# A graph transformer layer on one core: query exponentials straight from PSUM, count windows regrouped, second-layer weights rounded in pieces

## The chip, the cores and the metric

The kernel runs on one core of one Trainium2 chip. The metric is the time of one execution on the device in microseconds (us), lower is better.

## The reference

x is 1250 nodes of 768 features; 40000 edges with a source, a destination and one of three relations. All is float32. Cut to what matters:

```
xn = layernorm(x)
# relational graph attention, twice; layer 1 has 4 heads of 192, layer 2 has 1 of 768
xr = einsum('nd,rdf->rnf', x, W);  qi = xr[etype, dst] @ q;  kj = xr[etype, src] @ k
alpha = leaky_relu(qi + kj, 0.2)
e = exp(alpha - segment_max(alpha, dst)[dst]);  a = e / (segment_sum(e, dst)[dst] + 1e-16)
out = segment_sum(a * xr[etype, src], dst) + b
gnn = layer2(elu(layer1(xn)))
# linear attention of 12 heads of 64
q, k, v = xn @ W_qkv + b_qkv;  phi(x) = where(x > 0, x + 1, exp(x))
kv = sum_n phi(k) v^T;  y = phi(q) kv / max(phi(q) . sum_n phi(k), 1e-6)
mix = y @ W_out + b_out
x = x + gnn + mix
# int8 feed-forward
x = x + (clip(round(layernorm(x) / 0.02), -128, 127) @ weight_t) * 0.0002 + bias
```

## The kernel before

The nodes are ten blocks of 128 rows, the last one short; the features are six slices of 128 (`K6`). A float32 product is made of three float16 ones: each operand is split in a high part, made on ACT, and a low part, made on DVE, and a product of one block with 384 columns (`CW`) is 6 slices x 3 = 18 matmuls. The graph is turned into counts: for each relation, source and destination the number of edges, kept as 60 **count windows** of 21 destinations. A window is a chain of 14 matmuls of one-hot matrices (`count_window`, L1824), whose one-hots DVE builds in pairs (`one_hots`, L1345 and L1346, seven pairs a window); ACT copies the counts out of PSUM (`window_out`, L956) and SP stores them. First tile and count of a window are registers that PE and DVE each load from a table in memory (`window`, L446 to L452). The windows are spread over the stages as filling work; with the windows, `wq_tile` (L1885, 12 small matmuls) makes products of the graph weights with the attention vectors.

The stages in order: layernorm and transposes; K, then V (`W_K`, `W_V`; one window behind each product, L1824); K^T V (L1867); the **query stage**; a transition; the **y stage**; 20 **O products** (y @ W_out) followed by layer 1's products (both L1995), with masks and maxima beside them; layer 1's aggregation (L2044); **layer 2**'s 60 products in six chunks m = 0 to 5 (L1811 to L1813); its aggregation (L2101, L2102); the feed-forward.

The order within a stage is written out by hand for each engine; semaphores tie the engines together.

Query stage: six groups, each of 128 query features of all nodes in four row groups of 320 (`NRG`, `RG`), one PSUM bank each. A group runs over six k; a k step is 12 matmuls of 320 columns (L1911). Windows stand ahead of k = 2, of k = 4 and behind the group; a tile ahead of some k. PE loads the registers of the group's three windows at its start. When a bank is full (`q_done`), DVE adds the bias into `q_t` (L1451) and frees the bank (`q_free`), ACT makes exp(min(q, 0)) by Relu and Exp (L994, L996), and DVE combines both into `QF` (L1456). In the second half of the stage DVE also adds `bsum` = bo + b2 to the rows of X (L1461, L1462), and SP stores these to `acc_d` in the y stage (L642), from where they are loaded as the addend of the O products (`load_o`, L510; added at L1508).

After the last group PE does that group's third window and one more, then the y stage: per block `weighted` (12 matmuls of phi(q) with kv, L1925), DVE's division (`normalised`, L1468, L1472, L1477), PE's transposes of the result (L1936) and the two float16 parts (ACT, and DVE at L1490). Blocks 0 to 7 have a window, each block a tile.

Layer 2: per product ACT writes the high part of the result (L1168), DVE the low part (L1668, which frees the bank); in m = 1 to 3 DVE also makes two maxima per pair of blocks (L1676, L1679). Weights are double buffered: `w_hi_part` (L937, ACT) at the end of chunk m rounds the weights of chunk m + 2 in one piece, having waited for their load (`w_in`), and `w_lo_part` (L1371, DVE) makes the low part of chunk m + 1 behind the first pair of m. The aggregation's weights (`exponentials2`, `weights_part`, POOL's `pl` at L921) begin after the last product.

## Time and profile before

| | us |
|---|---|
| median of 3 runs | 1757.9 (1757.42, 1757.9, 1764.39) |
| profiled execution, device time | 1760.24 |
| its span in the trace | 1758.5 |
| busy: PE | 1621.5 (92% of the span) |
| busy: DVE | 1308.4 (74%) |
| busy: ACT | 774.4 (44%) |
| busy: POOL | 138.1 (8%) |

The mean granted clock of TensorE is 0.966 of full speed, and 183.30 MB pass through the DMA queues. In the rows below a line of a timeline or of the chain begins with the start and the length in us; "[3.03 <-PE ps L1911]" means that the engine had been idle for 3.03 us and what ended that; in a list of waits the numbers are the total in us, how often, and the longest. Matmuls overlap in the pipeline, so the length of one is more than its share of PE; the distance of two starts is the time that the work between them took. "x14" joins fourteen instructions in one row.

### The profile page before, as it was taken

How to read it: one execution, taken by the hardware profiler on the slowest of the kernel's cores; microseconds unless marked ns; L12 is line 12 of the kernel's file. 1: busy time of each engine (PE TensorE's matmuls, PEld its weight loads, DVE VectorE, ACT ScalarE, POOL GpSimd, SP SyncE). 2: the span in 40 equal slices, each digit the busy share in tenths (PEclk: the TensorE clock that was granted, in tenths of full speed). 3: DMA queues.
4: the chain of work that ended last, by engine and by line, in shares of the span. 5: the costliest groups of instructions: out<-in, count | busy, mean ns of one | idle time of the engine just before them, and what ended most of it. 6: DMA issues, size and time to landing. Idle time of an engine off the chain costs nothing.

```text
span 1758.5 us, 34402 instructions
## 1 busy us (share of the span) xinstructions
PE 1621.5 (92%) x10547; PEld 1179.7 (67%) x10548; DVE 1308.4 (74%) x2631; ACT 774.4 (44%) x1021; POOL 138.1 (8%) x245
## 2 busy tenths in 40 slices
PE   4999999987999999889999999989889799999987
PEld 3566667766755666469999999986555455555544
DVE  8698875578749999248899898973664377777785
ACT  4331112222234555168888898863211133333342
POOL 2000000000000000000000000000000033333340
PEclk8999999999899999989999999989999999999999
DMA  5111133323557664541003132132654541011212
GB/s 197 32 58 59 61 73 117 102 79 98 163 157 236 195 194 150 154 128 59 30 30 116 61 110 61 51 98 79 196 171 150 182 154 53 1 53 53 65 55 88
DMA packets 130308, 183.30 MB, mean 104 GB/s; under 512 B 14934, under 2 KB 100088, under 8 KB 130220
## 3 DMA queue, kind: packets, MB, share of 16 engines
q1 hardware_dynamic: 130220, 182.17, 33.4%
q8 instruction: 49, 0.80, 0.2%
q14 instruction: 39, 0.32, 0.1%
HBM read 121.33 MB, written 60.81 MB: 104 GB/s over the span
## 4 chain that ended last, share of the span: by engine, by line
PE 75%; DVE 10%; issue 5%; DMA 3%; ACT 3%; DVEq 2%; POOL 1%; SPq 1%; ACTq 0%; POOLq 0%
PE ps L2044 22%; PE ps L1995 12%; PE ps L2102 7%; PE ps L2101 7%; PE ps L1811 5%; PE ps L1813 4%; PE ps L1812 4%; PE ps L1824 4%; PE ps L1911 2%; PE ps L1885 2%; DVE oh_q L1345 2%; DVE oh_p L1346 1%; PE ps L2113 1%; PE ps L1980 1%; DMA xr_d<-ev 1%
## 5 line engine op out<-in xcount | busy, mean ns | idle before, releaser
L2044 PE MATMUL ps<-xrh,pf 128*128 (+1 forms) x2400 | 399.9, 329 | 11.3 <-DVE pf L1622 11.3
L2044 PEld LDWEIGHTS ps<-xrh,pf 128*128 128x128 f32 x2400 | 393.5, 191 | 17.8 <-issue 15.4
L1811 PE MATMUL ps<-w_hi,xt_hi 128*128 128x384 f16 x600 | 199.6, 333 | 23.9 <-DVE ev L1668 15.4
L1345 DVE TENSOR_SCALAR oh_q<-pat,codeT,neg_w 125x630 f16<-125x630 uint16 x420 | 185.8, 442 | 41.3 <-PE ps L1824 29.7
L1618 DVE SCALAR_TENSOR_TENSOR vb<-vb,tb 128x1260 f32<-128x1260 f32 x120 | 172.9, 1467 | 54.7 <-ACT vb L1119 53.8
L2101 PE MATMUL ps<-x,ph 128*128 (+1 forms) x600 | 196.5, 327 | 16.8 <-POOL pl L921 10.8
L1622 DVE SCALAR_TENSOR_TENSOR pf<-vb,CT 128x1260 f32<-128x1260 f32 x120 | 175.8, 1468 | 35.3 <-PE ps L2044 35.3
L1812 PE MATMUL ps<-w_lo,xt_hi 128*128 128x384 f16 x600 | 199.2, 332 | 0.0
L1813 PE MATMUL ps<-w_hi,xt_lo 128*128 128x384 f16 x600 | 199.1, 332 | 0.0
L2102 PE MATMUL ps<-x,ph 128*128 (+1 forms) x600 | 197.9, 330 | 0.0
L1119 ACT ACTIVATE vb<-qbc,kcol 128x1260 f32<-128x1260 f32 x120 | 161.0, 1345 | 39.5 <-DVE pf L1622 38.1
L1529 DVE CUSTOM_DVE_ANT_0 tt_junk<-kbc,mb 126x1260 bf16<-126x1260 f32 x120 | 169.1, 1466 | 10.0 <-issue 10.0
L1114 ACT ACTIVATE tb<-qbc,kcol_leak 128x1260 f32<-128x1260 f32 x120 | 159.6, 1343 | 20.2 <-DVE vb L1618 18.9
L1824 PE MATMUL ps<-oh_q,oh_p 125*128 125x315 f16 x840 | 132.1, 304 | 23.7 <-DVE oh_p L1346 23.1
L1181 ACT ACTIVATE ph<-p 128x252 f16<-128x252 f32 x150 | 61.9, 413 | 161.5 <-PE ps L2102 158.5
L921 POOL TENSOR_TENSOR pl<-p,ph 128x252 f16<-128x252 f32 x150 | 111.1, 742 | 197.4 <-ACT ph L1181 186.0
L1995 PE MATMUL ps<-w_hi,xt_hi 128*128 128x384 f16 x360 | 118.9, 330 | 7.4 <-ACT ev L1043 7.4
L1824 PEld LDWEIGHTS ps<-oh_q,oh_p 125*128 125x128 f16 x840 | 80.9, 99 | 66.3 <-DVE oh_p L1346 20.1
L1995 PE MATMUL ps<-w_lo,xt_hi 128*128 128x384 f16 x360 | 118.7, 330 | 0.0
L1995 PE MATMUL ps<-w_hi,xt_lo 128*128 128x384 f16 x360 | 118.5, 329 | 0.0
L1668 DVE TENSOR_TENSOR ev<-ps,ev 128x384 f16<-128x384 f32 x60 | 32.8, 556 | 101.1 <-ACT ev L1168 97.9
L1811 PEld LDWEIGHTS ps<-w_hi,xt_hi 128*128 (+1 forms) x600 | 59.7, 99 | 68.7 <-issue 32.4
(235 smaller groups left out, 2451.1 us busy)
## 6 DMA issues: line engine op xcount, KB each, us to landing
qbc<-tq_d SPq DMA_DIRECT2D x12, 1260.0 KB, 6.6
wst<-in_L_gnn_W SPq DMA_DIRECT2D x60, 192.0 KB, 3.2
xr_d<-ev SPq DMA_DIRECT2D x60, 192.0 KB, 2.0
xrh<-xr_d SPq DMA_DIRECT2D x4, 2880.0 KB, 14.8
x_d<-ev SPq DMA_DIRECT2D x60, 192.0 KB, 2.3
mb_d<-mb SPq DMA_DIRECT2D x30, 310.1 KB
mb<-mb_d SPq DMA_DIRECT2D x30, 310.1 KB
x<-x_d SPq DMA_DIRECT2D x2, 3840.0 KB, 18.9
```

The costliest lines, as they stand in the source:

```text
L1345: dve.tensor_scalar(oh_q[0:ET, u, :], pat[0:ET, :], codes[:, k:k + 1], neg_w[0:ET, ds(w, 1)], ALU.subtract, ALU.is_equal)
L1529: dve.tensor_tensor_reduce(out=tt_junk[k][0:WK, :], in0=kbc[0:WK, h, :], in1=mb[w % 2][0:WK, :], scale=1.0, scalar=2 * BIG, op0=ALU.subtra ...
L1618: dve.scalar_tensor_tensor(vb[j][:, :], vb[j][:, :], 2.0, tb[j][:, :], ALU.min, ALU.max).then_inc(v_step, 1)
L1622: dve.scalar_tensor_tensor(pf[j][:, 0:ND].rearrange("p (w d) -> p w d", d=WN), vb[j][:, :].rearrange("p (w d) -> p w d", d=WN), 2.0, CT[:, ...
L1811: pe.matmul(ps[:, bank, 0:CW], a_hi, hi[:, k, :], start=(k == 0), stop=False)
L1812: pe.matmul(ps[:, bank, 0:CW], a_hi, lo[:, k, :], start=False, stop=False)
L1813: last = pe.matmul(ps[:, bank, 0:CW], a_lo, hi[:, k, :], start=False, stop=(k == K6 - 1))
L1824: last = pe.matmul(ps[:, bank + q, 0:QH], oh_p[0:ET, u, :], oh_q[0:ET, u, q * QH:(q + 1) * QH], start=start, stop=False, skip_group_check= ...
L1995: mm = pe.matmul(ps[:, 6 + n % 2, 0:CW], a[:, k, i * P:(i + 1) * P], w[:, k, :], start=(q % PM == 0), stop=(q % PM == PM - 1))
L2044: mm = pe.matmul(out[b], pf[j][:, b * DB:b * DB + P], x, start=(first and b % 2 == 0), stop=False, skip_group_check=True)
L2101: pe.matmul(ps[:, bank, 0:CW], p, cols(off, off + CW), start=start, stop=False, skip_group_check=True)
L2102: mm = pe.matmul(ps[:, bank + 1, 0:CW + n1], p, cols(off + CW, off + D + n1), start=start, stop=False, skip_group_check=True)
```

## The change

1. **Query exponentials.** ACT reads the PSUM bank itself: Relu(-q - bq), then Exp; DVE makes `QF` in one operation, max(q + (bq + 1), exp), and only this frees the bank (`q_out` in place of `q_free`). `q_m` has four buffers, `q_t` is gone. The identity used: phi(q) = max(q + 1, exp(min(q, 0))).
2. **Biases.** `bsum` and its additions to X are gone, and so are the ten stores of X and the waits for them. POOL splits bo + b2 in three bfloat16 rows, which go through memory (`ob_d`) to `orow`; a matmul of ones with these three rows stands ahead of each O product. `load_o` reads x.
3. **Windows and tiles.** A query group has four windows, ahead of k = 2, 4 and 5 and behind the group (24 in place of 19 before the y stage); three blocks of the y stage have one, eight before. At a k the tile now stands ahead of the window, and groups 1 to 5 begin with one.
4. **K and V.** DVE loads a window's registers ahead of the wait for the product.
5. **Layer 2's weights.** In m = 1 to 4, ACT rounds those of chunk m + 1 in three pieces of two slices, behind its pairs 0, 1 and 2; DVE makes the low pieces behind its pairs 1, 2 and 3. Nothing is rounded at a chunk's end.
6. **Last aggregation.** Its first weights are made by DVE, ACT and POOL in and right after the last pair of m = 5.

The diff, cut to its core:

```diff
-W_A = W_Q + 3 * K6 + 1
-
-Q_TILES = (0, 3, 8, 13, 18, 22, 26)
+W_A = W_Q + 4 * K6
+
+Q_TILES = (0, 2, 7, 12, 17, 22, 27)
...
 def block_tiles(i):
...
-    return range(Q_TILES[-1] + i, Q_TILES[-1] + i + 1)
+    return range(Q_TILES[-1] + i, min(Q_TILES[-1] + i + 1, WT_TILES))
...
 def step_tile(q, k):
...
-    t = Q_TILES[q + 1] - K6 + k
-    return range(t, t + 1) if t >= Q_TILES[q] else range(0)
-
-assert W_A + NB >= NWN and block_tiles(NB - 1)[-1] == WT_TILES - 1
+    t = Q_TILES[q] + (k - 3 if q == 0 else k)
+    return range(t, t + 1) if Q_TILES[q] <= t < Q_TILES[q + 1] else range(0)
...
-    sp.dma_start(oa[n % 4][:, :], acc_d[i * P:(i + 1) * P, c * CW:(c + 1) * CW]).then_inc(oa_in[n % 4], 16)
+    rows = P if i < NB - 1 else TAIL
+    sp.dma_start(oa[n % 4][0:rows, :], x[i * P:i * P + rows, c * CW:(c + 1) * CW]).then_inc(oa_in[n % 4], 16)
...
     chunk_load(7)
+    sp.wait_ge(ob_step, 6)
+    sp.dma_start(ob_d.rearrange("j (p c) -> p j c", c=K6), osplit[:, :, :]).then_inc(ob_st, 16)
     for q in range(K6):
-        for k in range(1, K6):
+        for k in range(K6):
             if k in (3, 5):
...
+                store_window(sp, W_Q + 4 * q + k // 2 - 1, cc_, (4 * q + k // 2 - 1) % 2)
             for t in step_tile(q, k):
                 wq_load(t + 3)
-        store_window(sp, W_Q + 3 * q + 2, cc_, (3 * q + 2) % 2)
-    store_window(sp, W_A - 1, cc_, (W_A - 1 - W_Q) % 2)
+        for u in (2, 3):
+            store_window(sp, W_Q + 4 * q + u, cc_, (4 * q + u) % 2)
+        if q == 0:
+            sp.wait_ge(ob_st, 16)
+            sp.dma_start(orow[:, :], ob_d[:, :]).then_inc(or_in, 16)
     for i in range(NB):
-        sp.wait_ge(xb_done, i + 2)
...
     pool.wait_ge(bias_in, 80)
-    pool.tensor_tensor(bsum[:, :], bsum[:, :], b2_bc0[:, :], ALU.add).then_inc(xb_done, 1)
+    pool.tensor_tensor(ocol[:, :], ocol[:, :], o2col[:, :], ALU.add).then_inc(ob_step, 1)
...
         k = w - W_Q
         window_out(w, 6, cc_, k % 2, k // 2 + 3 * NB // 2 + (1 if k % 2 else 2))

+    act.wait_ge(bq_done, 1)
     for c in range(2):
         for fb in range(3):
-            wa = W_Q + 3 * (3 * c + fb)
-            late_out(wa)
-            late_out(wa + 1)
+            wa = W_Q + 4 * (3 * c + fb)
+            for u in range(3):
+                late_out(wa + u)
             for g in range(NRG):
                 n = (3 * c + fb) * NRG + g
-                act.wait_ge(q_free, n + 5)
-                act.wait_ge(q_out, n + 1)
-                act.activation(q_m[g % 2][:, :], q_t[g % 2][:, :], ACT.Relu, scale=-1.0).then_inc(q_mm, 1)
+                act.wait_ge(q_done, n + 1)
+                if n >= NRG:
+                    act.wait_ge(q_out, n - NRG + 1)
+                act.activation(q_m[g][:, :], ps[:, g, 0:RG], ACT.Relu, bias=nbq[:, 3 * c + fb:3 * c + fb + 1], scale=-1.0).then_inc(q_mm, 1)
                 act.wait_ge(q_mm, n + 1)
-                act.activation(q_m[g % 2][:, :], q_m[g % 2][:, :], ACT.Exp, scale=-1.0).then_inc(q_ee, 1)
-            late_out(wa + 2)
+                act.activation(q_m[g][:, :], q_m[g][:, :], ACT.Exp, scale=-1.0).then_inc(q_ee, 1)
+            late_out(wa + 3)
         w_hi_part(C_O + c)
-
...
             act.wait_ge(p_done, n + j + 3)
             act.wait_ge(mm_done, n + j + 1)
             act.activation(ph2[j][:, 0:GW], p2[j][:, :], ACT.Copy).then_inc(phi_done, 1)
+
+    for m in range(2 * R):
+        c = C_2 + m + 1
+        if 1 <= m < 2 * R - 1:
+            with act.Fori(0, 3) as ii:
+                x2_hi(m, ii)
+                act.wait_ge(w_in[c % 2], 16 * loads_to(c))
+                weights_free(act, c - 2)
+                act.activation(w_hi[c % 2][:, ds(2 * ii, 2), :], wst[c % 2][:, ds(2 * ii, 2), :], ACT.Copy).then_inc(w_hi_done, 1)
+            with act.Fori(3, NB // 2) as ii:
+                x2_hi(m, ii)
+        else:
+            with act.Fori(0, NB // 2 - 1) as ii:
+                x2_hi(m, ii)
+            if m == 2 * R - 1:
+                exp_v(0, 0, 0)
+            x2_hi(m, NB // 2 - 1)
+    p_hi(0, 0, 0)
...
+                    of_w = window(dve, W_V + 2 * (c * (NB // 2) + ii) + j + 1)
                     dve.wait_ge(g_done, n + 1)
...
             if i0 == 0:
...
     dve.wait_ge(ct_out[0], 16 * (3 * NB // 2 + 2) + 16)
...
     for c in range(2):
-        if c == 1:
-            dve.wait_ge(xb_done, 1)
         with dve.Fori(0, 3) as fb:
-            for u in range(2):
-                count_part(W_Q + 3 * (3 * c + fb) + u + 1)
+            for u in range(3):
+                count_part(W_Q + 4 * (3 * c + fb) + u + 1)
             for g in range(NRG):
                 n = (3 * c + fb) * NRG + g
-                dve.wait_ge(q_done, n + 1)
-                dve.wait_ge(q_out, n + 1)
-                dve.tensor_scalar(q_t[g % 2][:, :], ps[:, g, 0:RG], sub(bq_col, 3 * c + fb), None, ALU.add).then_inc(q_free, 1)
-                if g % 2:
-                    for g2 in (g - 1, g):
-                        n2 = (3 * c + fb) * NRG + g2
-                        dve.wait_ge(q_ee, n2 + 1)
-                        dve.scalar_tensor_tensor(sub(QF, 3 * c + fb)[:, g2 * RG:(g2 + 1) * RG], q_t[g2 % 2][:, :], 0.0, q_m[g2 % 2][:, :],
-                                                 ALU.max, ALU.add).then_inc(q_out, 1)
-            count_part(W_Q + 3 * (3 * c + fb) + 3)
-            if c == 1:
-                for u in range(3):
-                    dve.tensor_tensor(sub(X, 3 * fb + u), sub(X, 3 * fb + u), bsum[:, :], ALU.add).then_inc(xb_done, 1)
-    dve.tensor_tensor(X[:, NB - 1, :], X[:, NB - 1, :], bsum[:, :], ALU.add).then_inc(xb_done, 1)
+                dve.wait_ge(q_ee, n + 1)
...
-    count_part(W_A)
     for i in range(NB):
...
+    def low_piece(c, k):
+
+        dve.wait_ge(w_hi_done, parts_to(c - 1) + k + 1)
+        weights_free(dve, c - 2)
+        dve.tensor_tensor(w_lo[c % 2][:, ds(2 * k, 2), :], wst[c % 2][:, ds(2 * k, 2), :], w_hi[c % 2][:, ds(2 * k, 2), :],
...
+                p_v(0, 0, 0)
             with dve.Fori(i0, i1) as ii:
-                for j in range(2):
-                    dve.wait_ge(xr_hi, m * NB + 2 * ii + j + 1)
-                    dve.tensor_tensor(ev2[j][:, 0, :], ps[:, 6 + j, 0:CW], ev2[j][:, 1, :], ALU.subtract).then_inc(g_free, 1)
+                x2_lo(m, ii)
...
-            if i0 == 0 and m + 1 < 2 * R:
-                w_lo_part(C_2 + m + 1)
+                    maxima2(m, ii)
+            if i0 == 0 and m == 0:
+                w_lo_part(c)
         if m == 2 * R - 2:
...
         for fb in range(3):
-            wa = W_Q + 3 * (3 * c + fb)
-            of_w = [window(pe, wa + u)[1:] for u in range(3)]
+            wa = W_Q + 4 * (3 * c + fb)
+            of_w = [window(pe, wa + u)[1:] for u in range(4)]
             for k in range(K6):
-                if k in (2, 4):
-                    count_window(wa + k // 2 - 1, 6, *of_w[k // 2 - 1])
                 for t in step_tile(3 * c + fb, k):
                     if t == 0:
                         pe.wait_ge(kvd_done, 2)
                         pe.wait_ge(qkn_in, 64)
                     wq_tile(t)
+                if k in (2, 4, 5):
+                    count_window(wa + k // 2 - 1 + (k == 5), 6, *of_w[k // 2 - 1 + (k == 5)])
                 w_h, w_l = w_hi[cc % 2][:, k, fb * P:(fb + 1) * P], w_lo[cc % 2][:, k, fb * P:(fb + 1) * P]
                 for step, (w, t) in enumerate(((w_h, xt_hi), (w_h, xt_lo), (w_l, xt_hi))):
                     for g in range(NRG):
                         n = (3 * c + fb) * NRG + g
-                        if k == 0 and step == 0:
-                            pe.wait_ge(q_free, n + 1)
+                        if k == 0 and step == 0 and n >= NRG:
+                            pe.wait_ge(q_out, n - NRG + 1)
                         last = pe.matmul(ps[:, g, 0:RG], w, t[:, k, g * RG:(g + 1) * RG], start=(k == 0 and step == 0),
                                          stop=(k == K6 - 1 and step == 2))
                         if k == K6 - 1 and step == 2:
                             last.then_inc(q_done, 1)
-            count_window(wa + 2, 6, *of_w[2])
-
-    of_w = window(pe, W_A - 1)[1:]
-    count_window(W_A - 1, 6, *of_w)
-    pe.wait_ge(q_out, 2 * 3 * NRG + 2)
...
             a = t_lo if step == 2 else t_hi
-            mm = pe.matmul(ps[:, 6 + n % 2, 0:CW], a[:, k, i * P:(i + 1) * P], w[:, k, :], start=(q % PM == 0), stop=(q % PM == PM - 1))
+            if c < C_X and q % PM == 0:
+                pe.matmul(ps[:, 6 + n % 2, 0:CW], one3[:, :], orow[:, (c - C_O) * CW:(c - C_O + 1) * CW], start=True, stop=False)
```

How the change stands in the order of instructions, at three places. First PE between two query groups (w_hi_84, w_lo_86 are a chunk's weights, oh_q and oh_p the one-hots, wt a tile's weights, tabrow the table of windows). Before:

```order
L1824 MATMUL ps<-oh_q,oh_p 128x315 x6
L1833 ISA
L1833 REGISTER_ALU
L1833 COMPARE_AND_BRANCH
L1839 MATMUL ps<-zrow,ident_50 128x2
L448 TENSOR_LOAD tabrow
L448 ISA x2
L448 TENSOR_LOAD tabrow
L448 ISA x2
L448 TENSOR_LOAD tabrow
L448 ISA x2
L1911 MATMUL ps<-xt_hi,w_hi_84 128x320 x4
```

and with the change:

```order
L1913 MATMUL ps<-zrow,ident_50 128x2
L454 TENSOR_LOAD tabrow
L454 ISA x2
L454 TENSOR_LOAD tabrow
L454 ISA x2
L454 TENSOR_LOAD tabrow
L454 ISA x2
L454 TENSOR_LOAD tabrow
L454 ISA x2
L1959 MATMUL ps<-qkn,wt_114 128x2x4 x6
L1985 MATMUL ps<-xt_hi,w_hi_90 128x320 x4
L1985 MATMUL ps<-xt_lo,w_hi_90 128x320 x4
```

A fourth load stands ahead of the group, and a tile ahead of its first k step; L1824 and L1913 (before L1839) close the window ahead of it.

Second DVE at the end of the query stage, from the last one-hots to the first normalisation of y. Before:

```order
L1346 TENSOR_SCALAR oh_p<-iota_l,sloT 125x128
L1356 ISA
L1356 REGISTER_ALU
L1356 COMPARE_AND_BRANCH
L1461 ISA
L1461 TENSOR_TENSOR X<-X,bsum 128x768
...
L1462 TENSOR_TENSOR X<-X,bsum 128x768
L1468 TENSOR_SCALAR rdn_107<-ps 128x6 x2
L1472 RECIPROCAL rdn_107<-rdn_107 128x12
L1477 TENSOR_TENSOR yn_105<-ps,rdn_107 128x384 x2
L448 TENSOR_LOAD tabrow
```

and with the change:

```order
L1400 TENSOR_SCALAR oh_p<-iota_l,sloT 125x128
L1410 ISA
L1410 REGISTER_ALU
L1410 COMPARE_AND_BRANCH
L1499 REGISTER_ALU
L1499 COMPARE_AND_BRANCH
L1513 TENSOR_SCALAR rdn_112<-ps 128x6 x2
L1517 RECIPROCAL rdn_112<-rdn_112 128x12
L1522 TENSOR_TENSOR yn_110<-ps,rdn_112 128x384 x2
```

The additions of bsum to X between the two are gone, and no window (L448) stands behind the first normalisation.

Third DVE in layer 2, one pair of blocks of m = 1 (ev is a bank's two halves, mk and mkt the maxima). Before, the first pair and what stands behind it:

```order
L1668 TENSOR_TENSOR ev_0_127<-ps,ev_0_127 128x384
L1668 TENSOR_TENSOR ev_1_128<-ps,ev_1_128 128x384
L1675 MEMSET tick 128x1
L1676 ISA tt_junk_0_207,mk_0_216<-kbc_204,mb_0_205 126x1260
L1676 ISA mk_0_216 126x1
L1679 COPY mkt<-mk_0_216 126x1
...
L1665 REGISTER_ALU
L1665 COMPARE_AND_BRANCH
L1371 TENSOR_TENSOR w_lo_86<-wst_82,w_hi_84 128x2304
L1665 UNCONDITIONAL_BRANCH
L1665 ISA
L1668 TENSOR_TENSOR ev_0_127<-ps,ev_0_127 128x384
```

and with the change, the second pair, in the loop:

```order
L1709 TENSOR_TENSOR ev_0_132<-ps,ev_0_132 128x384
L1708 REGISTER_ALU
L1709 TENSOR_TENSOR ev_1_133<-ps,ev_1_133 128x384
L1725 REGISTER_ALU
L1727 ISA x2
L1727 TENSOR_TENSOR w_lo_91<-wst_87,w_hi_89 128x768
L1715 ISA
L1716 ISA
L1717 MEMSET tick 128x1
L1718 ISA tt_junk_0_212,mk_0_221<-kbc_209,mb_0_210 126x1260
L1718 ISA mk_0_221 126x1
```

The low part of 2304 columns behind the first pair is gone; one of 768 stands within each of three pairs, behind the subtractions that free the banks and ahead of the maxima.

## Rows read from the trace of the kernel before

**Rows 1.** table of stretches: us, busy of each engine (instructions), clock, DMA
```profile
414.00:472.00 58.00, 52.31 (x417) 45.69 (x415) 54.80 (x184) 14.81 (x29) 2.20 (x9) 0.96 0.47 142
...
1172.00:1200.00 28.00, 20.94 (x258) 17.22 (x259) 18.75 (x37) 20.06 (x33) 0.00 (x0) 0.64 0.32 107
```

**Rows 2.** waits of PE in 40 to 258 us, of DVE in 72 to 258
```profile
PE ps L1824 <- DVE oh_p L1346: 7.0, 8, 3.1
...
DVE oh_q L1345 <- issue: 7.3, 16, 0.6
```

**Rows 3.** timeline of 258 to 276 us, query stage: start, length, engine, line, operation
```profile
267.43 2.08 PE L1824 MATMUL ps<-oh_q,oh_p 125*128 125x315 f16 x14
268.38 0.45 DVE L1345 TENSOR_SCALAR oh_q<-pat,codeT,neg_w 125x630 f16<-125x630 uint16 x1 [3.85 <-PE ps L1824]
...
269.38 1.48 PE L1885 MATMUL ps<-qkn,wt 128*128 128x8 f32 x12
...
270.72 0.70 PE L1911 MATMUL ps<-xt_hi,w_hi 128*128 128x320 f16 x4
...
271.49 0.44 DVE L1345 TENSOR_SCALAR oh_q<-pat,codeT,neg_w 125x630 f16<-125x630 uint16 x1
...
272.34 1.40 PE L1885 MATMUL ps<-qkn,wt 128*128 128x8 f32 x12
...
275.12 1.01 DVE L1451 TENSOR_SCALAR q_t<-ps,bq_col 128x320 f32<-128x320 f32 x2 [3.03 <-PE ps L1911]
```

**Rows 4.** register loads of L448: shortest, median, longest ns
```profile
L448 PEldq TENSOR_LOAD <-tabrow x60: 295/302/564, 71.8 to 460.7; - x60
```

**Rows 5.** timeline of 299 to 304 us, one group's exponentials
```profile
300.22 1.01 DVE L1451 TENSOR_SCALAR q_t<-ps,bq_col 128x320 f32<-128x320 f32 x2 [3.03 <-PE ps L1911]
...
300.80 0.47 ACT L994 ACTIVATE q_m<-q_t 128x320 f32<-128x320 f32 x1 [5.43 <-DVE q_t L1451]
...
301.92 0.49 DVE L1456 SCALAR_TENSOR_TENSOR QF<-q_t,q_m 128x320 f32 x1 [0.69 <-ACT q_m L996]
```

**Rows 6.** timeline around the last drain (DVE) and y's first transposes (PE)
```profile
402.64 1.01 DVE L1451 TENSOR_SCALAR q_t<-ps,bq_col 128x320 f32<-128x320 f32 x2 [3.03 <-PE ps L1911]
...
418.14 0.87 PE L1936 MATMUL ps<-ident,yn 128*128 128x128 f32 x6 [1.65 <-DVE yn L1477]
```

**Rows 7.** timeline of PE, 466 to 472 us, the last y blocks
```profile
466.46 0.85 PE L1936 MATMUL ps<-ident,yn 128*128 128x128 f32 x6
...
470.85 0.92 PE L1936 MATMUL ps<-ident,yn 128*128 128x128 f32 x6 [0.97 <-DVE yt_lo L1490]
```

**Rows 8.** chain that ended last, 36 matmuls; timeline of PE, a stall
```profile
572.72 5.85 PE ps L1995 x36
...
541.89 0.50 PE L1995 MATMUL ps<-w_hi,yt_hi 128*128 128x384 f16 x1 [2.40 <-DVE oa L1508]
```

**Rows 9.** the chain to layer 2's end: last matmuls of m = 0 and 4
```profile
1228.26 0.17 PE ps L1813
...
1361.25 0.18 PE ps L1813
```

**Rows 10.** waits of ACT in 1200 to 1400 us
```profile
ACT w_hi L937 <- DMA wst<-in_L_gnn_W: 18.2, 4, 5.9
```

**Rows 11.** timeline of 1258 to 1278 us, DVE in m = 1 and 2
```profile
1261.74 0.56 DVE L1668 TENSOR_TENSOR ev<-ps,ev 128x384 f16<-128x384 f32 x1 [0.62 <-ACT ev L1168]
...
1262.22 1.47 DVE L1676 CUSTOM_DVE_ANT_0 tt_junk<-kbc,mb 126x1260 bf16<-126x1260 f32 x1
...
1265.66 0.15 DVE L1679 COPY mkt<-mk 126x1 f32 x1
...
1272.99 2.56 DVE L1371 TENSOR_TENSOR w_lo<-wst,w_hi 128x2304 f16<-128x2304 f32 x1
```

**Rows 12.** timeline of PE at the last aggregation's start
```profile
1402.29 0.48 PE L2101 MATMUL ps<-x,ph 128*128 128x384 f16 x1 [5.96 <-DMA x<-x_d]
```

**Rows 13.** waits of ACT in 258 to 402.5 us
```profile
ACT cc L956 <- PE ps L1839: 82.4, 12, 10.0
```

More of the change, by code:

```diff
@@ L157, in build @@
         yt_lo = place("yt_lo", [P, K6, NPAD], F16, 159984 + 15360)
-        q_t = [place(f"q_t{j}", [P, RG], F32, 129024 + 1280 * j) for j in range(2)]
-        q_m = [place(f"q_m{j}", [P, RG], F32, 131584 + 1280 * j) for j in range(2)]
+        q_m = [place(f"q_m{j}", [P, RG], F32, 70656 + 1280 * j) for j in range(NRG)]
         kvd = place("kvd", [P, K6, AW], F32, 134144)
@@ L1196, in _ @@
                     if g < NG - 1 or r < 2:
-                        with act.Fori(0, NB // 2) as ss:
+                        with act.Fori(1 if g == 0 and r == 0 else 0, NB // 2) as ss:
                             exponentials2(g, r, ss)
@@ L2000, in _ @@
             pe.wait_ge(ct_ev, NWN + 1)
+            pe.wait_ge(or_in, 16)
             product_steps(0, PM)
```

170 lines of the change are left out of this document (108 added, 62 removed).

## The prediction

> **What bounds the kernel now.** The table of stages comes first: the tensor engine (PE) is busy for 52.31 of the 58 us of the stage that makes y, at a granted clock of 0.96, and in the short stage of transposes before the second layer for 20.94 of 28 us, at 0.64 [rows 1]. PE has work nearly everywhere, so a change can pay in three ways: less work on PE, fewer stalls of PE, or less DVE time where PE waits for DVE. So I read next who stalls PE, and whether DVE stands still for nothing visible [rows 2], then the timeline of the query stage [rows 3 to 5], of the transition behind it [rows 6] and of the y blocks [rows 7], and the chain and waits of the O products and of layer 2 [rows 8 to 11]. All sums are made against the profiled execution, 1760.24 us. The median of the runs is 2.3 lower, 1757.9, and the number at the end is on that scale.
>
> **K and V stage.** DVE now loads a window's registers before it waits for the product, not after. Before the first one-hot DVE stands 7.3 us for nothing visible, in 16 places, at most 0.6 in one [rows 2]: that is the register work. It pays only where DVE is the late one, and there PE waits for one-hots 7.0 us in 8 places [rows 2]. So the gain is between 0 and 7.0. Those waits are near the chunks' starts, where a few windows in a row are paced by DVE; five of them at about 0.5 give **-2.5**.
>
> **Query groups.** A group of query features has six k steps, four or five tiles of wq_tile, and three count windows, now four. The units: a window 1.95 us (267.43 to 269.38), a tile 1.34 (269.38 to 270.72), a k step 1.62 (270.72 to 272.34) [rows 3]. A group is then 6 x 1.62 + 3 x 1.95 + 5 x 1.34 = 22.3; the measured period, from one drain to the next, is 300.22 - 275.12 = 25.1 [rows 3, 5], so 2.8 of it are stalls: register loads on PE's own sequencer, late one-hots, banks freed late. With a fourth window the work is 24.2. Two things can stall it. First, four register loads of 0.302 [rows 4] and the splitting of their words, near 2.0 us, which PE can only begin when the last window's matmuls are issued; those come late, since DVE needs 0.52 for a pair of one-hots (268.38 to 271.49 is six pairs [rows 3]) and has seven pairs to make. I take 1.2 of the 2.0 as showing. Second, a bank is now held until DVE has combined it: two ACT operations of 0.47 for each of four row groups, then 0.49 on DVE [rows 5], 4.3 us for the last. PE wants that bank after a window (1.95), the loads and the tile that now stands first (1.34), 4.5 us with the loads that show. So the tile and the window hide it; without them PE would wait some 3 us per group. Sum 24.2 + 1.2 = 25.4, 0.3 more than now, five times, and 1.3 for the first group, which had a stall less: **+2.8**. Ends: all stalls gone, 6 x -0.9 = -5; all stalls kept, 6 x 1.95 = +12. I take the value near the lower middle, since the order of tiles and windows covers both stalls.
>
> The 24 additions of the bias from PSUM (1.01 for two [rows 3]) leave DVE, 2.0 a group, and a window's one-hots, seven pairs at 0.52, come: 1.6 more on DVE per group, which stays below PE's 25. Nothing.
>
> The page "DMA: Bandwidth & Descriptors" of the Trainium skill (section "Latency and other measured facts") gives a register load from memory a floor of about 600 ns. The row has 302 in the median and 564 at most [rows 4], so it goes against the page; by the page four loads would show 1.2 us more at each of five group starts, 6 us, and the sum below would be -17.
>
> **From the last query group to y.** From the last drain, 402.64, to the first transposes of y, 418.14, are 15.5 us [rows 6]. In them PE has to run two windows ahead of y's first weighted products, and DVE makes the one-hots of the second only after it has combined the group; behind them it has four sums X + bsum ahead of the first normalisation. Now PE has one window there, whose one-hots are made before the exponentials, and goes on to the weighted products; the sums are gone; one set of one-hots, for the window behind, still stands ahead of the normalisation. The new path is DVE's: exponentials and combination of four row groups, 4 x 0.94 + 0.49 = 4.3; one-hots and their registers, 7 x 0.52 + 0.5 = 4.1; a normalisation, some 1.9. 10.3: **-5.2**. It is 0 if both sets of one-hots still stand on the path, -9 if those one-hots hide too.
>
> **The y blocks.** Eight blocks with a count window take 466.46 - 418.14 = 48.3 us [rows 6, 7], 6.04 each; a block without one takes 470.85 - 466.46 = 4.39 [rows 7]. Five blocks lose their window: 5 x 1.65 = **-8.2**. This is the other side of the fourth window: moved from a place where it costs 1.65 to one where it costs up to 1.95, and the last group's and the transition's stalls are what is won.
>
> **O products.** The bias comes as a matmul of three rows and 384 columns ahead of each of 20 products, at 5.85 / 36 = 0.1625 as any other [rows 8]: 3.2 us. PE has a stall of 2.40 behind DVE among them [rows 8], which takes in a part: **+2.2**; ends 0 and 3.2. On SP's queue the stores of X and the wait for them leave; the loads of the addend can start earlier, which PE does not wait for: nothing. The bias's splitting on POOL, its store and its load have the whole query stage as cover; were that gone, PE would stand before the first O product. The sums X + bsum on DVE leave the query stage's second half, where PE does not wait for them: nothing.
>
> **Layer 2.** From the end of chunk m = 0 to that of m = 4 are 1361.25 - 1228.26 = 133.0 us [rows 9]. Ten products of 18 matmuls are 5 x 5.85 = 29.25 [rows 8], four chunks 117.0, so 16.0 are stalls: ACT stands 18.2 us in 4 places for the load of the weights that it rounds [rows 10], with the next chunk's x2_hi queued behind it and x2_lo and PE's bank behind that; and the low part, 2.56 in one piece on DVE [rows 11], holds up x2_lo. In pieces, ACT rounds a chunk only behind the first pair of the chunk before it, some 5.85 us later than now; the longest wait is 5.9, so the load is there or nearly, and both stalls go. In exchange three pairs of each chunk carry a low piece, 2.56 / 3 and a fixed part, 0.95 by my estimate. In m = 1 to 3 such a pair has on DVE two subtractions of 0.56, the piece, and two maxima of 1.47 with their small operations, 3.6 [rows 11]: 5.7, and some 0.3 of registers, against 5.85 that PE gives a pair. PE becomes late by a little at each piece and once at the end, 1.3 a chunk, 3.9 in three; m = 4 has no maxima, none. **-12.1**; ends -16.0 and 0.
>
> **Start of the last aggregation.** PE is released at 1402.29, after 5.96 us, by the transfer of x_d [rows 12], not by the weights that the change makes earlier. **0.** Were the transfer quick, the weights would be late next, and the change has them ready.
>
> **Sum:** -2.5 + 2.8 - 5.2 - 8.2 + 2.2 - 12.1 = -23.0. 1760.2 - 23.0 = 1737.2, on the median's scale 1735; rounded down a little for the low ends that I left at nothing (DVE's lighter query stage, SP's shorter queue), 1734.
>
> **Rivals.**
> (a) *The clock falls in the y blocks without windows.* Blocks 3 to 9 are then short transposes and weighted products. The stage of that kind before layer 2 has a clock of 0.64, the y stage with windows 0.96 [rows 1]. Of a block's 4.39 about 2 us are transposes and weighted products that the chain waits for; at the lower level (1.2 GHz) they double, and the 0.97 that PE idles now [rows 7] takes up a third of that: +1.5 a block, six blocks 9 us, 1743. Against it: the one such block in the rows is quick, though it is the first behind windowed ones. The Trainium skill's page "TensorE: Matmul & The Clock Gate" (Part 1) calls the throttled clock the default and says that activity lifts it, which is on this rival's side. Chance 0.17.
> (b) *The pieces cost nothing and the group starts hide.* Layer 2 gains 16.0, the query stage -3: ten more, 1724. Chance 0.15.
> (c) *DVE becomes the bound in layer 2.* If every one of twelve pieces holds PE up by 1.0, as where it waits for ACT's high piece with the maxima queued behind it, the gain is 16 - 12 = 4, 8 less: 1742. Chance 0.10.
> (d) *Slower.* The bank is freed at the end of ACT then DVE, and ACT's queue holds the copy of the window before, which waits for the store of an earlier window. If that store is late, the exponentials, the combination and the bank are late behind it, at every group start. The kernel is slower once a group start costs 24 / 5 = 4.8 us; at 6 us it is 1764. Against it: this copy waits for PE alone, 82.4 us in 12 places, never for a transfer [rows 13]. Chance 0.03.
> (e) *The windows are not what makes the y blocks long.* A block without one then stays at 6.0 and 8 us are not won: 1742. The row of the short block speaks against it. Chance 0.04.
>
> **How the numbers follow.** My forecast has the remaining 0.51. The range 1718 to 1750 takes in the forecast with the ends of its terms, (a), (b), (c) and (e); beyond it lie (d) and two of (a), (c), (e) together above, and several low ends together below, under 0.2 in all. A measurement of this kernel can tell about 0.5% (8.8 us) from no change, so faster means below 1749.1: the forecast and each of (a), (b), (c), (e) alone, 0.91. Two of them together end near 1751: same 0.06. Slower is (d), 0.03.
>
> **What would show it.** Right: 25 to 26 us from drain to drain in the query stage; 10 to 11 from the last to y's first transposes; y blocks 3 to 8 at 4.4 with a clock above 0.9; layer-2 chunks m = 1 to 3 near 30.5 and m = 4 near 29.3; no wait of ACT for weights there; the aggregation still released by x_d. Wrong: a clock near 0.6 in the y stage; PE waiting at group starts for combined features; PE waiting for x2_lo in each pair of layer 2.

## The result and the profile after

The changed kernel takes 1768.9 us (median of 20 runs, 1761.8 to 1775.7) against 1758.1 (20 runs, 1753.7 to 1769.1): ratio 1.0052, 95% interval 1.0036 to 1.0067, so slower by about 0.5%. Forecast was 1734, with a range of 1718 to 1750. The profiled execution took 1769.05 us, its span 1767.3 at a mean clock of 0.954 (before 1758.5 and 0.966).

Where it went, from the first and last rows of each stage's matmuls in the two timelines; the last column is the prediction's term:

| stretch | before | after | difference | forecast |
|---|---|---|---|---|
| to the first query matmul | 250.2 | 249.0 | -1.2 | -2.5 |
| query stage, to its last matmul | 152.4 | 175.4 | **+23.0** | +2.8 |
| from there to y's first transposes | 15.5 | 10.1 | -5.4 | -5.2 |
| y's transposes, first to last | 53.4 | 51.4 | **-2.0** | -8.2 |
| to the last O matmul | 87.5 | 94.1 | **+6.6** | +2.2 |
| layer 1's products | 200.1 | 198.0 | -2.1 | 0 |
| to layer 2's last product | 636.6 | 626.3 | -10.3 | -12.1 |
| from there to the end | 362.8 | 363.0 | +0.2 | 0 |

Three rows hold 30.8 of the 31.8 us between this difference (+8.8) and the forecast (-23.0): the query stage 20.2, y 6.2, the O products 4.4. The table of stretches of the changed kernel (length, busy time of PE, its weight loads, DVE, ACT, POOL, granted clock, share and rate of the DMA) shows what they have in common. Its rows here are the query stage, the transition and the end of the y stage:

```profile
249.00:424.40 175.40, 162.14 (x1100) 122.90 (x1101) 102.76 (x366) 36.00 (x66) 4.61 (x14) 0.86 0.33 96
424.40:434.50 10.10, 4.39 (x30) 3.12 (x27) 8.51 (x29) 6.20 (x10) 0.00 (x0) 0.77 0.10 34
...
466.50:488.50 22.00, 19.78 (x96) 19.30 (x96) 10.98 (x26) 4.11 (x10) 0.00 (x0) 0.52 0.06 19
```

The same for the kernel before:

```profile
250.00:402.60 152.60, 135.79 (x1002) 101.49 (x1000) 98.20 (x319) 31.65 (x59) 2.76 (x6) 0.96 0.38 106
```

A mean clock of 0.86 over 175.4 us is 24.6 us' worth of work lost, 0.96 over 152.6 is 6.1. By this estimate some 18 of the 23 us in the query stage are clock. What stands ahead of its falls is in the list of PE's waits in 250 to 424.4 us (total, how often, the longest), and in the chain of waits around a group's start:

```profile
PE ps L1959 <- issue: 10.1, 5, 2.1
```

The chain there (start, length, what):

```profile
272.26 1.96 PE ps L1898 x14
274.22 0.01 PE ps L1913
274.23 2.00 issue
276.22 2.67 PE ps L1959 x12
278.89 3.21 PE ps L1985 x12
282.10 2.36 PE ps L1959 x12
284.46 3.21 PE ps L1985 x12
287.67 2.36 PE ps L1959 x12
290.03 3.59 PE ps L1898 x14
293.62 0.00 PE ps L1913
293.62 1.65 PE ps L1985 x12
```

The group's last window (L1898) ends, PE stands for 2.00 us with nothing to wait for but its own sequencer, and comes back at the lower level (1.2 GHz): a tile takes 2.4 to 2.7 us for 1.24, a k step 3.21 for 1.65. It stays there for some 16 us of unbroken work, until the next window has run (a k step at 293.62 takes 1.65 again).

The five starts did not all go this way, with the same order of work at each. The timeline of PE shows the second without a fall: the tile takes 1.50 and the last four matmuls of the k step 0.71. The third and fourth fall at once, and so does the fifth, but at the third the clock is back after some 4 us and at the fifth after some 7, both ahead of any window:

```profile
310.57 1.50 PE L1959 MATMUL ps<-qkn,wt 128*128 128x8 f32 x12 [2.00 <-issue]
313.01 0.71 PE L1985 MATMUL ps<-xt_hi,w_lo 128*128 128x320 f16 x4
...
336.78 1.86 PE L1959 MATMUL ps<-qkn,wt 128*128 128x8 f32 x12 [2.06 <-issue]
338.49 1.23 PE L1985 MATMUL ps<-xt_hi,w_hi 128*128 128x320 f16 x4
...
342.67 0.70 PE L1985 MATMUL ps<-xt_hi,w_hi 128*128 128x320 f16 x4
```

The rows of the register loads say why PE stood: of the four loads behind the first group (L454, 0.30 each, and some 0.3 for the splitting of each word) the first starts at 273.6 and the last ends its splitting at 276.1, while the window's matmuls were all started by 274.1.

```profile
L454 PEldq TENSOR_LOAD <-tabrow x4: 295/298/309, 273.6 to 275.5; - x4
```

### The profile page after: what moved, and what is told of

Its sections match the earlier page's. It is cut to its first block, busy times and chain, and to the rows that moved or that the text cites. A ratio compares the mean times of both kernels' runs of the same rounds, so it can differ in the third digit from the quotient of the medians.

```text
span 1767.3 us, 34410 instructions
## 1 busy us (share of the span) xinstructions
PE 1643.8 (93%) x10567; PEld 1200.1 (68%) x10568; DVE 1288.6 (73%) x2605; ACT 776.7 (44%) x1029; POOL 140.3 (8%) x254
## 4 chain that ended last, share of the span: by engine, by line
PE 81%; DVE 7%; issue 4%; DMA 3%; ACT 2%; DVEq 1%; POOL 1%; SPq 0%; ACTq 0%; POOLq 0%
PE ps L2119 21%; PE ps L2069 13%; PE ps L2177 7%; PE ps L2176 7%; PE ps L1898 6%; PE ps L1885 5%; PE ps L1886 4%; PE ps L1887 4%; PE ps L1985 3%; PE ps L1959 3%; PE ps L2188 1%; PE ps L1997 1%; PE ps L2052 1%; DMA xr_d<-ev 1%; PE ps L1941 1%
## 5 line engine op out<-in xcount | busy, mean ns | idle before, releaser
L2119 PE MATMUL ps<-xrh,pf 128*128 (+1 forms) x2400 | 399.4, 329 | 11.3 <-DVE pf L1666 11.3
L1666 DVE SCALAR_TENSOR_TENSOR pf<-vb,CT 128x1260 f32<-128x1260 f32 x120 | 175.7, 1467 | 34.9 <-PE ps L2119 34.9
L1898 PE MATMUL ps<-oh_q,oh_p 125*128 125x315 f16 x840 | 132.2, 307 | 6.8 <-DVE oh_p L1400 6.3
L1898 PEld LDWEIGHTS ps<-oh_q,oh_p 125*128 125x128 f16 x840 | 82.9, 102 | 47.0 <-DVE oh_p L1400 8.3
L1400 DVE TENSOR_SCALAR oh_p<-iota_l,sloT 125x128 f16<-125x128 f16 x420 | 103.2, 246 | 0.0
L1747 DVE SCALAR_TENSOR_TENSOR p<-v,CT 128x252 f32<-128x252 f32 x150 | 69.6, 492 | 45.2 <-ACT v L1205 43.4
```

The lines of the kernel that those rows point to most:

```text
L1666: dve.scalar_tensor_tensor(pf[j][:, 0:ND].rearrange("p (w d) -> p w d", d=WN), vb[j][:, :].rearrange("p (w d) -> p w d", d=WN), 2.0, CT[:, ...
L1898: last = pe.matmul(ps[:, bank + q, 0:QH], oh_p[0:ET, u, :], oh_q[0:ET, u, q * QH:(q + 1) * QH], start=start, stop=False, skip_group_check= ...
L2119: mm = pe.matmul(out[b], pf[j][:, b * DB:b * DB + P], x, start=(first and b % 2 == 0), stop=False, skip_group_check=True)
```

## The experiments

All times are medians, and ratios are to the kernel before on the same chip. e1 to e4 shared one chip (before: 1760.1), e5, e6, e8 and e9 a second (1760.5), e10 to e12 a third (1756.3), and e13 had a fourth (1760.4), so differences between these sets carry a chip's offset. A trace is of one execution; where that one is the highest or lowest of its kernel's times, the text says so.

**e1: the loads apart.**

```diff
-of_w = [window(pe, wa + u)[1:] for u in range(4)]
+of_w = {}
 for k in range(K6):
...
+    if k in (1, 3, 4, 5):
+        u = (k + 1) // 2 - 1 if k < 4 else k - 2
+        of_w[u] = window(pe, wa + u)[1:]
```

> The changed kernel, with the four register loads of a query group no longer together at its start but one each ahead of k = 1, 3, 4 and 5. Theory A (the loads): PE's standstill of 2.00 us at each of five group starts (10.1 us in all) goes, and with it the falls of the clock that follow it (about 48 us at the lower level in the query stage of the changed kernel, 14 in that of before): 15 to 27 us less than the changed kernel, so 1742 to 1754, faster than before. Theory B (the work): the fourth window and the tiles make the stage long and lower the clock by themselves; the standstill goes, 10 us less, the low clock stays: 1757 to 1761.

1736.3 us, ratio to before 0.9861 (0.9832 to 0.9890): some 33 us less than the changed kernel for moving twenty-four register loads. It is more than theory A asked for, whose range ended at 1742. In the trace the query stage is 146.4 us long between the first and last of its low-part products (174.3 in the changed kernel), no standstill by the sequencer is left (the banks hold PE up for 1.7 us in all), and the clock is 0.98 (table of stretches):

```profile
248.00:395.50 147.50, 142.20 (x1104) 108.81 (x1102) 103.30 (x372) 36.49 (x66) 4.27 (x14) 0.98 0.38 115
```

**e2: more loads in the kernel before.**

```diff
 of_w = [window(pe, wa + u)[1:] for u in range(3)]
+for u in range(3):
+    window(pe, wa + u)
```

> The kernel before, with three more register loads on PE at each query group's start (results unused). Theory A: each start gets up to 2.0 us of standstill more (three loads of 0.5 with their splitting behind the three that were hidden under a window), six times, and the clock falls behind some: 8 to 25 us slower than before, with more than 14 us at the lower clock in the query stage. Theory B: loads are hidden under matmuls already issued: less than 3 us slower, low clock time unchanged.

1757.9 us, 0.9983 (0.9962 to 1.0003): no cost, where theory A had 8 to 25 us. PE does stand, up to 1.68 us at a start, but in 1.09 of it would have waited for the bank anyway, and the waits for one-hots go from 10.6 to 8.0 us, nearly what the starts cost more (8.3 for 5.4, and 1.9 ahead of the first group). The clock in the query stage is 0.96 as before. The list of PE's waits there, and the timeline of PE around one start:

```profile
PE ps L1913 <- DVE q_t L1451: 8.3, 5, 1.7
```

```profile
303.73 0.17 PE L1839 MATMUL ps<-zrow,ident 128*128 128x2 f16 x1
305.58 0.71 PE L1913 MATMUL ps<-xt_hi,w_hi 128*128 128x320 f16 x4 [1.68 <-DVE q_t L1451]
```

So neither the number of loads nor a standstill of 1.7 us is enough in this kernel. One thing that differs is what comes next: a k step of 320 columns here, a tile of 8 columns in the changed kernel.

**e3: layer 2's pieces and the early aggregation weights alone, on the kernel before** (the changed lines for these two, nothing else).

> The kernel before, with only the pieces of the second layer's weights and the early first aggregation weights. Both theories on the query stage are silent; from the changed kernel's trace the stretch from the last layer-1 product to the end of layer 2's products is 10.3 us shorter and the aggregation's start unchanged: 10 us faster than before, 1748. If 10.3 was luck of the clock: 0 to 5 us faster.

1746.5 us, 0.9925 (0.9899 to 0.9952): 13 us less, with an interval of 8 to 18 that holds the 10 expected.

**e4: the windows back.** The changed kernel with three windows a group, one ahead of y and eight in the y blocks.

```diff
-W_A = W_Q + 4 * K6
+W_A = W_Q + 3 * K6 + 1
...
-if k in (2, 4, 5):
+if k in (2, 4):
```

> The changed kernel, with windows where they were before (three per query group, one ahead of y, eight in y's blocks) and three register loads per start; the exponentials, bias, tiles, pieces and K/V order stay as changed. Theory A: three loads with an early third window are hidden as before; y's blocks keep their clock: query stage back near 150 us, transition back to 14 or 15, y 53, O products 88: 1738 to 1750. Theory B': the new exponentials, which free banks late, are what makes the group starts long: query stage stays over 160 us: 1758 or more.

1730.4 us, 0.9837 (0.9806 to 0.9868), with e9 the fastest that keeps the whole result, and below theory A's 1738 to 1750, which had the query stage near 150 us. The query stage (first to last low-part product) is 133.6 us against 151.3 before, with the same windows: a group is 22.4 us, the bare sum of its work. Of the stalls before, 5.4 for banks and 10.6 for one-hots, 2.4 and 3.9 are left (the list of PE's waits), and the clock is 0.99.

```profile
PE ps L1900 <- DVE oh_p L1401: 3.9, 3, 3.1
PE ps L1987 <- DVE QF L1506: 2.4, 5, 0.5
```

**e5: the tile behind k = 0.** The changed kernel; only the first tile of groups 1 to 5 moves behind the matmuls of k = 0.

> The changed kernel, with the tile that stood first in groups 1 to 5 put behind the matmuls of k = 0; the four loads stay together at the start. Theory C (the stall alone): the standstill of 2.0 us stays at each start and the clock falls as before, 1762 to 1770, over 35 us at the lower clock in the query stage. Theory D (the stall and the tile together): the tile's matmuls of 8 columns next to the standstill are what keeps the clock down; with 12 matmuls of 320 columns there instead the clock stays or is back at once: under 20 us low, 1745 to 1757. A bank wait of up to 1 us may appear at each start.

1765.5 us over 10 runs (1753.0 to 1770.4), 0.9999 (0.9970 to 1.0027): the median lies in theory C's range, four of the ten runs lie in theory D's or just above it (1753.0 to 1759.5), and the ratio is some 0.5% below the changed kernel's. The trace is of the highest of the ten times; there the clock of the stage is 0.86, as low as in the changed kernel. The edit had put the tile of k = 0 right ahead of that of k = 1, 24 matmuls of 8 columns in a row, so it is no fair test of theory D (chain of waits, group 2's start):

```profile
277.52 2.28 PE ps L1985 x12
279.80 4.92 PE ps L1959 x24
```

One thing it does tell. The clock falls in the k step right behind the standstill, ahead of the tiles, and so it does at four of the five starts. The timeline of PE, first and last four matmuls of that k step:

```profile
277.52 0.71 PE L1985 MATMUL ps<-xt_hi,w_hi 128*128 128x320 f16 x4 [2.00 <-DVE QF L1505]
...
278.61 1.19 PE L1985 MATMUL ps<-xt_hi,w_lo 128*128 128x320 f16 x4
```

So a tile next to the standstill is not needed for a fall.

**e13: tiles from k = 1.** The edit that e5 should have been: five tiles ahead of k = 1 to 5, loads at the start, never two tiles together.

```diff
-t = Q_TILES[q] + (k - 3 if q == 0 else k)
+t = Q_TILES[q] + (k - 3 if q == 0 else k - 1)
```

> The changed kernel, with the five tiles of groups 1 to 5 ahead of k = 1 to 5 instead of 0 to 4: four loads at the start, then directly the 12 matmuls of k = 0, and never two tiles side by side (as they stood in the kernel with the tile behind k = 0, where the clock fell as in the changed one). Theory D (standstill and tile side by side bring the clock down, and tile, k, tile, k keeps it there): it falls less, under 25 us low in the query stage, a standstill or bank wait of 2.0 at each start stays: 1745 to 1755. Theory C (the standstill alone): over 35 us low, 1760 or more.

1752.2 us, 0.9953 (0.9929 to 0.9976), 1.0% under the changed kernel's ratio. PE stands as long and as often as in the changed kernel, 10.1 us in five places, the longest 2.1. The profile puts this down to the bank, but at the first of the five DVE had freed that bank at 272.91, the loads end at 275.3 and PE starts at 275.38, so it is the loads. In the trace, which is of the lowest of the twelve times (1747.9), the clock is 0.96 instead of 0.86 and the stretch 157.7 instead of 175.4 us; the whole execution's mean clock is 0.968 there and 0.961 in the median of the runs (changed kernel: 0.953), so the typical gain is smaller. List of PE's waits, and table of stretches:

```profile
PE ps L1985 <- DVE QF L1505: 10.1, 5, 2.1
```

```profile
248.50:406.20 157.70, 144.83 (x1101) 111.79 (x1102) 102.92 (x368) 36.00 (x66) 4.62 (x14) 0.96 0.38 107
```

Same standstill, same work, and the place of the tiles decides some 1.0%: theory D's time holds. Its mechanism holds in part. The clock still falls at two of the five starts, within the k step (at the fourth the first four matmuls take 1.06 us), but no fall lasts longer than some 7 us. And e13 changes two things at once: the tile leaves the standstill's side, and two tiles instead of three stand ahead of the group's first window. e5 has the k step beside the standstill as well, three tiles behind it, and falls like the changed kernel, which points to the second; no run parts them fully.

```profile
356.78 1.06 PE L1985 MATMUL ps<-xt_hi,w_hi 128*128 128x320 f16 x4 [2.00 <-DVE QF L1505]
```

**e10: two of four loads at the start.**

> The changed kernel, with two of the four register loads at a group's start and one each ahead of k = 4 and 5: a smaller dose of the same standstill. PE should stand about 1.0 us at each of five starts. If the clock answers to the length of the standstill, it stays up behind 1.0 us as it did behind the 1.09 us of the kernel before: 1736 plus 5, 1741, under 20 us low in the query stage. If any standstill at that place brings it down: over 30 us low, 1750 to 1760.

1754.1 us, 0.9981 (0.9960 to 1.0002): 18 us more than with none (across two chips). PE stands 3.6 us in five places, the longest 0.8, ahead of the tile, and the clock is 0.90. The expectation that a standstill of this length leaves the clock up is refuted: one a third as long brings it down too, at four of the five starts. In all it stays down for less time (0.90 over 163.5 us against 0.86 over 175.4), so the length is not without effect. The timeline of PE at the second start shows a fall within the k step behind the tile: the k step's first four matmuls are shown at 0.70 us, its last four at 1.27.

```profile
300.87 0.17 PE L1913 MATMUL ps<-zrow,ident 128*128 128x2 f16 x1
301.71 1.50 PE L1959 MATMUL ps<-qkn,wt 128*128 128x8 f32 x12 [0.68 <-issue]
303.07 0.70 PE L1987 MATMUL ps<-xt_hi,w_hi 128*128 128x320 f16 x4
303.61 0.74 PE L1987 MATMUL ps<-xt_lo,w_hi 128*128 128x320 f16 x4
304.15 1.27 PE L1987 MATMUL ps<-xt_hi,w_lo 128*128 128x320 f16 x4
```

**e11: the four loads together, ahead of the group's last window.**

```diff
+last_w = of_w[3]
+if wa + 4 < W_A:
+    of_w = [window(pe, wa + 4 + u)[1:] for u in range(4)]
-count_window(wa + 3, 6, *of_w[3])
+count_window(wa + 3, 6, *last_w)
```

> The changed kernel, with the four loads of the next group still together, but ahead of the last window of the group instead of behind it. Theory A in its narrower form (not the number of loads, but that PE's sequencer reaches them only when the late one-hots of the fourth window let it, with nothing issued to cover them): they now run while PE works off k = 5, no standstill over 0.5 us at the starts, clock up: 1734 to 1740. If bunched loads stall wherever they stand: 1755 to 1769.

1739.3 us, 0.9898 (0.9874 to 0.9921). Bunched, but 0.2 to 0.8 us of standstill each is all that shows (2.7 in five places), since PE has the matmuls of k = 5 to work off meanwhile, and it lies ahead of a window, not of a tile (list of PE's waits):

```profile
PE ps L1898 <- issue: 2.7, 5, 0.8
```

The stage's clock is 0.94. What is low of it lies in the first group, ahead of any of the starts that the edit touches; e12 shows the same there (both 0.57 over 255 to 275 us), e1 and e4 a shorter fall. I take that for chance from run to run, and did not test it; both traces are of the highest of their kernel's times, which speaks for it.

**e8: the old places of the tiles**, on e4: behind the window at a k, none at k = 0.

> The kernel with the windows back, and also the tiles where they were before (behind the window at a k, none at k = 0), so that of the query stage only the exponentials are as changed. If the exponentials alone made the group short (22.4 us a group against 25.1 before): query stage within 3 us of 134.6, 1730. If the tile at the group's start is needed as cover for the banks: waits of 1.5 to 3 us at each of five starts, 1738 to 1745.

1735.3 us, 0.9856 (0.9821 to 0.9891), between the two expectations. The stage is 140.9 us, 7.3 more than e4 and 11.1 less than e3's 152.0: so the exponentials gave 11 and the tile at the start 7 in these traces. This one is of an execution of 1740.6 us, 5 above e8's median, and the medians of e8 and e4 are 5.0 apart, so 5 is nearer. It is also what the banks cost more, 7.4 us instead of 2.4 (list of PE's waits). Of the 11 some 5 are clock, 0.98 against e3's 0.94, which no run parts from chance:

```profile
PE ps L1987 <- DVE QF L1506: 7.4, 15, 0.6
```

**e9: e4 with its three loads apart.**

> The kernel with the windows back, with the three loads of a group spread ahead of k = 1, 3 and 5. If they are hidden under the third window as the trace says: same within 2 us, 1728 to 1731. If some stall of loads is left there: 3 to 8 us less.

1731.6 us, 0.9829 (0.9795 to 0.9862), e4 was 0.9837: no difference. Three loads behind a window whose one-hots are ready early were hidden, as in the kernel before, where they ran from 300.2 to 302.0 under the window at 300.33.

**e6: no bias matmul**, on e4 (the bias bo + b2 is left out of the output).

> The kernel with the windows back (1730.3), without the bias matmul ahead of the 20 O products, so bo + b2 is left out of the output. If each costs 0.1625 us: 3.2 us less, 1727. If part of it lay under DVE's pace as forecast: 2.2 less or under. If it costs more than its own length (a change of form in the chain): 5 or more less, 1725.

1728.7 us, 0.9821 (0.9788 to 0.9855); e4's interval covers it. In the traces the O products take 86.1 us (452.5 to 538.6) against 89.3 (452.4 to 541.7) in e4: 3.2 us, twenty times 0.16, so in these two traces all of it is on the path; the medians (1.7 apart, on two chips) can't confirm it.

**e12: nine windows in y's blocks**, on e4, none between the groups and y.

> The kernel with the windows back (1730.3), with the window ahead of y moved into y's blocks: nine of them have one. By the units: the transition goes from 13.2 to 10.1 us, y gains one window of 1.65: 1729. If the clock needs that window ahead of y: it falls in the transition and 3 to 5 us are lost: 1733.

1733.3 us, 0.9868 (0.9845 to 0.9892), e4 0.9837 (0.9806 to 0.9868) on another chip. The median is the second expectation's, but the clock does not fall in the transition, as that one had it: it is 0.99 there, and the transition takes the 10.2 us of the first. The long fall in this execution's first group hides what it is worth. Not settled.

## Why the prediction was wrong

**The step that failed** is the query groups' "I take 1.2 of the 2.0 as showing": 2.00 show at each of five starts (four us more), and a stall was priced at its own length. What the sum left out is the clock: it fell behind four of the five standstills, for up to 16 us of full work, with the tile that I counted as cover for the banks first in line. That is some 18 us. Together these are 22 for a miss of 20.2; the stage's other terms come out some 2 us better than forecast. Put side by side, the runs show it with the same 24 windows and 27 tiles (the clock is that of the one traced execution, the ratio of all runs):

| kernel | PE stands at five starts | next is | starts with a fall | clock, query stage | last minus first low-part product | ratio to before |
|---|---|---|---|---|---|---|
| e1 | 0, banks 1.7 | tile | 0 | 0.98 | 146.4 | 0.986 |
| e11 | 2.7, ahead of the window | window | 0 | 0.94 | 152.3 | 0.990 |
| e13 (lowest of its times) | 10.1 | k step | 2 | 0.96 | 156.6 | 0.995 |
| e10 | 3.6 | tile | 4 | 0.90 | 162.4 | 0.998 |
| changed | 10.1 | tile | 4 | 0.86 | 174.3 | 1.005 |
| e5 (highest of its times) | 10.1 | k step, then two tiles | 4 | 0.86 | 176.8 | 1.000 |

e1 against the changed kernel shows that the bunched loads bring the falls at the starts, and e10, e11 and e13 that their number and place decide what they cost. Why the clock, once down, stays down at one start and comes back at another with the same work stays open.

**Why the loads show at all.** I had them begin when the last window's matmuls were issued, and that was right. What I got wrong is how late that is: the fourth window's one-hots are ready at 273.16, the window ends 1.1 us later, and 2.6 us of loads and splitting stand behind. The third window of the kernel before had its one-hots long before, so the loads ran under its 1.9 us.

**The length of a load, and the clock's default.** I had weighed the Trainium skill's floor of about 600 ns for a register load (page "DMA: Bandwidth & Descriptors", section "Latency and other measured facts") and set it aside for the row's 302. The rows after have 300 again, so the row was the right duration; but the rest of a window's registers costs as much again, and per window the page's 600 happens to be nearer to what PE pays (2.0 to 2.6 us for four). For the clock, the Trainium skill's page "TensorE: Matmul & The Clock Gate" (Part 1) says that the throttled state is the default and activity releases it. The trace of the changed kernel agrees in part: work released it every time, but once only after some 16 us of tiles and k steps without a gap (from 276.22) and once after some 4 us of the same (from 336.78).

**What was mis-sized in the same stage.** "The 24 additions ... Nothing" hid a gain: with the additions and the sums gone and the bank read by ACT itself, the query stage lost 11 us (e8 against e3, some 5 of them clock), and 5 to 7 more with the tile at the start (e4 against e8). "Without them PE would wait some 3 us per group" was too much: without that tile e8 waits 7.4 us for banks in five starts, 1.5 each. The fourth window costs 12.8 (e1 against e4), 2.1 a group, forecast 1.95. Without the loads at the start the stage comes out at -4.9 instead of +2.8 (e1).

**The transition** was forecast at 10.3 and took 10.1. **The y blocks**: rival (a), at 0.17, is what happened. The three windowless blocks at 453.19 to 466.51 take 4.40, 4.46 and 4.46 as the row before had it; the later ones 5.60, 6.33 and 6.33, at 0.52 of the clock. Also the first block is 8.0 us for 6.06, since PE had stood 3.6 us and came back at the lower level. The timeline of PE, y's transposes:

```profile
453.19 0.85 PE L2008 MATMUL ps<-ident,yn 128*128 128x128 f32 x6
457.59 0.92 PE L2008 MATMUL ps<-ident,yn 128*128 128x128 f32 x6 [0.96 <-DVE yt_lo L1534]
462.05 0.92 PE L2008 MATMUL ps<-ident,yn 128*128 128x128 f32 x6 [0.96 <-DVE yt_lo L1534]
466.51 0.92 PE L2008 MATMUL ps<-ident,yn 128*128 128x128 f32 x6 [0.96 <-DVE yt_lo L1534]
472.11 1.52 PE L2008 MATMUL ps<-ident,yn 128*128 128x128 f32 x6
478.44 1.52 PE L2008 MATMUL ps<-ident,yn 128*128 128x128 f32 x6
484.77 1.52 PE L2008 MATMUL ps<-ident,yn 128*128 128x128 f32 x6
```

I had made (a) a rival of the y stage alone, at +1.5 a block, and never asked the same of the query stage, where the change adds standstills next to tiles. In e4, with a window in eight blocks, the stage's clock is 0.99. Up to the first O product it takes 56.0 us there and 51.8 in e1, so the windows' move wins 4.2 in the y stage, not 8.2, and 3.1 in the transition (13.2 to 10.1), and costs 12.8 in the groups: 5.5 us lost. The O products, which begin at the lower clock in e1, take 3.1 more there (92.7 against 89.6): 8.6 in these stretches. On one chip the median of e4 is faster than that of e1 by 6.0.

**O products**: the matmuls cost 3.2, not 2.2. The rest of the 6.6 I can divide only in part: the stretch starts at the lower clock, which y's last blocks left behind; without bias (e6) it is still 1.7 us longer than before.

**Layer 2** came out as worked out. ACT's wait for the weights, 18.2 us [rows 10], is 0.3 in the list of its waits:

```profile
ACT w_hi L1222 <- DMA wst<-in_L_gnn_W: 0.3, 1, 0.3
```

and from the last matmul of m = 0 to that of m = 4 are 1368.11 - 1246.45 = 121.7 us for 133.0 [rows 9]: -11.3, forecast -12.1. Timeline of PE:

```profile
1246.45 0.33 PE L1887 MATMUL ps<-w_hi,xt_lo 128*128 128x384 f16 x1
...
1368.11 0.33 PE L1887 MATMUL ps<-w_hi,xt_lo 128*128 128x384 f16 x1
```

The chunks m = 1 to 4 take 30.0, 30.8, 31.6 and 29.25 (forecast 30.5 three times, 29.3). Some 1.6 us are given back in m = 5, 36.5 for 34.9. Over layer 2 ACT now waits for stores of x_d for 20.6 us in 6 places, before 10.5 in 2; that this is why was not tested. **The aggregation's start** is still released by the transfer, as said [rows 12]:

```profile
PE ps L2176 <- DMA x<-x_d: 5.6, 1, 5.6
```

**K and V**: DVE's standstill before the first one-hot went from 7.3 us to 0.6, PE's waits for one-hots from 7.0 to 3.2 [rows 2]; the stage is 1.2 shorter, forecast 2.5. The lists of waits of PE (40 to 249 us) and of DVE (72 to 249):

```profile
PE ps L1898 <- DVE oh_p L1400: 3.2, 6, 1.1
```

```profile
DVE oh_q L1399 <- issue: 0.6, 1, 0.6
```

Had the loads been apart, the sum would have been met: e1 takes 1736.3, forecast 1734. The terms inside were off both ways: against before, e1's query stage is 7.7 us better than forecast (-4.9 for +2.8), and its y stage and O products some 9 worse (-4.7 for -8.2, +7.9 for +2.2). So that agreement is partly luck.

## What to carry to other kernels

Price a standstill of PE by the work behind it too, not by its length alone: here 10.1 us of standstill cost some 33 us by the medians (changed against e1), and some 16 with the tiles placed otherwise (e13 against e1, on two chips). A register load on PE's own sequencer was free here only while matmuls already issued covered it; put it ahead of work whose operands come late, not behind. And moving filling work out of a stage of small matmuls can cost it its clock: the last y blocks ran at 0.52 without windows, the same stage at 0.99 with them (e4).

## What the runs showed of the hardware

A standstill of 0.7 us ahead of a tile can be enough for a fall to 1.2 GHz (four of five starts, e10). One of 2.0 was followed by a fall at four of five starts ahead of a tile (changed kernel), and ahead of a k step at four of five (e5, in the highest of its times) and at two of five (e13, in the lowest). The same loads set apart, with bank waits of at most 0.4 us at the starts, were followed by none (e1). Once down, PE stayed at 1.2 GHz for some 16 us in which it was never idle at two starts of the changed kernel, tiles of few columns and k steps in turn, and was back after some 4 and 7 us at two others, with the same order of work. That the tiles lengthen the falls is my reading of e13 against e5 and the changed kernel; no run shows what decides how long one lasts, and it was not tried with other small matmuls.
